# Layer 0's tile pipeline with the heads' normalization behind the second top-k round and the row statistics behind the third

## What is computed

```
x = x + attention(norm(x)) @ Wo + bo                      # projection: this stage
Q = norm(x) @ Wq.T + bq                                   # 16 heads
scores = Q K / 4                                          # 77 columns per head
topk_scores = top_k(scores, 32); weights = softmax(topk_scores)
x = x + (weights @ V) @ Wo.T + bo
h = norm(x); probs = softmax(h @ router_w + router_b)
x = x + (h @ expert_w[argmax].T + expert_b[argmax]) * max(probs)
```

## Time and profile before

| | |
|---|---|
| median of 3 runs | 1985.16 us (1983.98 to 1985.93) |
| the profiled execution, device time | 1987.05 us |
| its span in the trace | 1985.3 us |
| PE, DVE, ACT, POOL busy over the span | 80%, 63%, 47%, 24% |
| the stage cross_experts | 583.5 to 1118.5 us of the span |
| first top-k round starts | 608.10 us |
| distance of two tiles' first rounds, steady part | 27.24 us |
| tile 15's first round starts | 1006.21 us |
| last instruction of the stage | 1115.44 to 1116.07 us |

### The profile page before, as it was taken

How to read it: one execution, slowest core, us unless ns; L and a number is a source line. 1 busy time by engine, 2 the same in 40 slices (tenths; PEclk the granted TensorE clock), 3 DMA queues, 4 the chain that set the end, 5 groups by cost and what they waited for, 6 DMA issues and landing times. The chain is left out here.

```text
span 1985.3 us, 27618 instructions
## 1 busy us (share of the span) xinstructions
PE 1579.4 (80%) x8891; PEld 871.2 (44%) x8892; DVE 1255.1 (63%) x4695; ACT 934.1 (47%) x1831; POOL 482.1 (24%) x386
## 2 busy tenths in 40 slices
PE   4758999999976488889867676999987882389993
PEld 2431222222224366767656432333326761156662
DVE  6988888887407999999980356777735558401112
ACT  2731777777655445555543340666673651111110
POOL 3760000000003354455542151111111342300003
PEclk9965999999897778888878785999998995689997
DMA  6175133331010000000000059336300121741003
GB/s 196 59 203 79 21 45 44 44 45 20 25 43 1 1 1 2 1 1 1 1 1 1 6 163 170 43 44 86 44 1 1 15 41 32 254 162 33 26 24 93
DMA packets 113013, 102.91 MB, mean 52 GB/s; under 512 B 45095, under 2 KB 88171, under 8 KB 112878
## 3 DMA queue, kind: packets, MB, share of 16 engines
q1 hardware_dynamic: 111345, 97.06, 22.6%
q0 software_dynamic: 1536, 4.20, 0.7%
HBM read 67.61 MB, written 33.35 MB: 51 GB/s over the span
## 5 line engine op out<-in xcount | busy, mean ns | idle before, releaser
L1052 DVE TENSOR_REDUCE arena<-banks 128x2 f32<-128x1024 f32 (+1 forms) x448 | 481.2, 1108 | 149.7 <-PE banks L899 94.3
L988 ACT ACTIVATE arena<-banks 128x512 f32<-128x512 f32 (+3 forms) x896 | 439.9, 557 | 187.3 <-PE banks L938 180.6
L899 PE MATMUL banks<-arena 96*128 96x512 bf16 (+3 forms) x896 | 285.9, 396 | 50.1 <-DVE arena L1052 21.2
L938 PE MATMUL banks<-arena 98*128 98x512 bf16 (+3 forms) x896 | 272.0, 364 | 9.0 <-ACT arena L988 6.8
L950 PE MATMUL banks<-arena 128*32 128x512 f32 (+3 forms) x1792 | 220.8, 565 | 12.6 <-ACT arena L988 6.5
L1654 DVE MATCH_REPLACE8 arena<-arena 128x77 f32<-128x77 f32 x1024 | 213.9, 226 | 0.0
L899 PEld LDWEIGHTS banks<-arena 96*128 96x128 bf16 x896 | 80.6, 102 | 233.7 <-DVE arena L1052 136.9
L938 PEld LDWEIGHTS banks<-arena 98*128 98x128 bf16 x896 | 82.4, 98 | 188.0 <-ACT arena L988 124.1
L2433 DVE COPY arena<-banks 128x1024 f32<-128x1024 f32 x23 | 28.2, 1225 | 206.9 <-PE banks L2372 206.9
L1549 POOL TENSOR_SCALAR arena<-arena 128x256 f32<-128x256 f32 x32 | 39.1, 1223 | 476.2 <-DVE arena L1635 476.1
L1650 DVE MAX8 arena<-arena 128x8 f32<-128x77 f32 x1024 | 149.5, 225 | 1.4
(11 more groups left out here) (276 smaller groups left out, 2535.2 us busy)
## 6 DMA issues: line engine op xcount, KB each, us to landing
arena<-parts SPq DMA_DIRECT2D x192, 128.0 KB, 7.3
arena<-in_L_ffn_W SPq DMA_DIRECT2D x16, 1024.0 KB, 12.2
parts<-arena SPq DMA_DIRECT2D x24, 512.0 KB, 9.1
v<-arena SPq DMA_DIRECT2D x32, 256.0 KB, 2.3
arena<-v SPq DMA_DIRECT2D x16, 512.0 KB, 11.1
arena<-sorted SPq DMA_DIRECT2D x23, 128.0 KB, 2.1
expert_out<-arena SPq DMA_DIRECT2D x23, 128.0 KB, 1.7
sorted<-arena SPq DMA_DIRECT2D x5, 512.0 KB, 7.4
```

Of the source, the lines that this page charges most:

```text
L899: mm = pe.matmul(bank[:, 0:w], qst[r][0:KS, j, i * P:(i + 1) * P], kst[r][0:KS, j, kb * BANK:kb * BANK + w], start=True, stop=not diag)
L938: pe.matmul(bank, kst[r][0:KM, j, kt * P:(kt + 1) * P], qst[r][0:KM, j, half * BANK + lo:(half + 1) * BANK], start=True, stop=True).then_i ...
L988: act.activation(prob[:, gi % 2 * G + j, lo:BANK], PS[:, 4 + n % 3, 0:BANK - lo], ACT.Exp, scale=SCALE).then_inc(sem(s + "_exp"), 1)
L1052: dve.tensor_reduce(m2[u % 2][:, 2 * pair:2 * pair + 2, i, kb], PS[:, 2 * (n % 2):2 * (n % 2) + 2, 0:w], AX.X, ALU.max).then_inc(sem(s + " ...
```

## The change

An iteration now touches fewer tiles: t+2 (projection, first normalization), t+1 (queries and scores), t (top-k), t-1 (weights, context, heads' normalization, output, second normalization and logits) and t-2 (choice and experts). The loop runs from -2 to 17, 20 iterations. To make that possible within an iteration,

- DVE has `largest` split in two (the 8 largest; `taken`, the replacing). Its order is now: round 1; router, choose, chosen of t-2; round 2; `sums` and `normalize` of t-1; round 3; row statistics, gates; round 4; `inverse`.
- PE turns the weights of t-1, then context, turn_context, then choice and spread of t-2, then turn_mixed and output of t-1, experts of t-2, turn_h1, turn_h2, logits.
- ACT's order follows PE's; `deviations`, `gated`, `turned_h1`, `turned_h2` end its iteration.
- POOL does d2, w, the subtraction for all scores, the spread, then h2, h1, the bias and the addition to x.
- The experts' sum moves to bank 1 (EB), the logits to bank 7; the waits that guard banks and buffers follow. `choose` uses a two-tensor subtraction for the one with a scalar pointer. The eight expert matrices are turned 3, 3 and 2 at a time in the first iterations, before 2 in each of four. No DMA is added, removed or moved.

The arithmetic for each tile is the same.

```diff
-            PB, WB, QB, OB = 3, 4, 6, 7
-            FIRST, LAST = -3, T + 4
+            EB, PB, WB, QB, OB = 1, 3, 4, 6, 7
+            FIRST, LAST = -2, T + 2
+            TURNS = (3, 3, 2)
...
-                return [w for w, n in ((0, t + 2), (1, t - 3)) if inside(n)]
+                return [w for w, n in ((0, t + 2), (1, t - 1)) if inside(n)]
...
-                    if inside(t - 4):
-                        turn_choice(t - 4)
-                        turn_spread(t - 4, 0)
-                        turn_spread(t - 4, 1)
+                    if inside(t - 1):
+                        for c in range(4):
+                            turn_weights(t - 1, c)
+                        context(t - 1)
+                        turn_context(t - 1)
                     if inside(t - 2):
-                        turn_mixed(t - 2)
...
+                        turn_choice(t - 2)
+                        for c in range(4):
+                            turn_spread(t - 2, c)
+                    if inside(t - 1):
+                        turn_mixed(t - 1)
+                        output(t - 1)
...
+                        experts(t - 2, 0)
+                        experts(t - 2, 1)
                     if inside(t + 2):
                         turn_h1(t + 2)
-                    if inside(t - 3):
-                        turn_h2(t - 3)
                     if inside(t - 1):
-                        context(t - 1)
-                    if inside(t - 3):
-                        logits(t - 3)
+                        turn_h2(t - 1)
+                        logits(t - 1)
...
-                    dve.tensor_scalar(ta[n], lg[n], m1[n], None, ALU.subtract).then_inc(sem(s + "_ta"), 1)
+                    dve.tensor_tensor(ta[n], lg[n], m1[n].to_broadcast([P, E]), ALU.subtract).then_inc(sem(s + "_ta"), 1)
...
                 for t in range(FIRST, LAST):
-                    if inside(t - 4):
-                        router(t - 4)
+                    if inside(t):
+                        largest(t, 0)
+                        taken(t, 0)
+                    if inside(t - 2):
+                        router(t - 2)
+                        choose(t - 2)
+                        chosen(t - 2)
+                    if inside(t):
+                        largest(t, 1)
+                        taken(t, 1)
+                    if inside(t - 1):
+                        sums(t - 1)
+                        normalize(t - 1)
+                    if inside(t):
+                        largest(t, 2)
+                    if inside(t):
+                        taken(t, 2)
                     if normed(t):
                         row_statistics(t)
-                    if inside(t - 4):
-                        choose(t - 4)
-                    if normed(t):
                         aggregate(t)
...
```

More of the change, by code:

```diff
@@ L1176, in steps, with turned @@
                 return sum(1 for n in range(FIRST, t + 1) if normed(n))
+            def turned(t):
+                n = t - FIRST
+                return range(sum(TURNS[:n]), sum(TURNS[:n + 1]))
             @block.sync
@@ L1350, in _ @@
                         query(t + 1)
[L1351 to L1354, removed]
+                    if inside(t + 2):
+                        turn_attended(t + 2)
                     if inside(t + 1):
                         scores(t + 1)
[L1357 to L1361, removed]
@@ L1375, in _ @@
[L1375 to L1382, removed]
+                    if inside(t + 2):
+                        project(t + 2)
+                    for e in turned(t):
+                        turn_expert(e)
@@ L1500, in _ @@
                         exp_left(t - 1)
-                    if inside(t + 3):
-                        attended(t + 3)
-                    if inside(t - 4):
-                        router_exp(t - 4)
+                    if inside(t + 2):
+                        attended(t + 2)
+                    if inside(t + 1):
+                        copy_scores(t + 1)
+                    if inside(t + 2):
+                        attended_rows(t + 2)
+                    for e in turned(t):
+                        act.wait_ge(sem(s + "_wep"), e + 1)
+                        act.copy(WeT[:, e].rearrange("p k n -> p (k n)"), PS[:, WB + e % 2, :]).then_inc(sem(s + "_weT"), 1)
@@ new lines, in _ @@
+                    if inside(t - 1):
+                        for c in range(4):
+                            copy_weights(t - 1, c)
+                        context(t - 1)
+                    if inside(t - 2):
+                        router_exp(t - 2)
+                    if inside(t):
+                        exp_all(t)
+                    if inside(t - 2):
+                        choice(t - 2)
+                        for c in range(4):
+                            copy_spread(t - 2, c)
@@ L1505, in _ @@
+                    if inside(t - 1):
+                        mixed(t - 1)
+                        mixed_rows(t - 1)
                     if normed(t):
                         deviations(t)
[L1507 to L1514 removed]
@@ L1540, in _ @@
                     if inside(t - 1):
-                        context(t - 1)
+                        turned_h2(t - 1)
             @block.gpsimd
@@ L1650, in largest, with taken @@
                         dve.max(m8[r][:, k, hd, :], src[:, hd, :]).then_inc(sem(s + "_m" if k == 0 else f"{s}_m{k}"), 1)
+                def taken(t, k):
+                    r, hn = t % 2, t * NH
+                    src = (sc if k == 0 else left)[r]
                     dve.wait_ge(sem(s + "_m" if k == 0 else f"{s}_m{k}"), hn + NH)
```

157 lines of the change are left out of this document (57 added, 100 removed).

## The result

The changed kernel takes 2039.5 us (median of 4 runs, 2036.96 to 2046.45) against 1985.07 us: **2.8% slower**, ratio 1.0278, 95% interval 1.0262 to 1.0294. Forecast were 2043.5 us, range 2012 to 2070, slower.

A forecast was written before the change was run, and what follows sets the result against it. PE and DVE were both taken as close to the limit, with DVE newly waiting for context. Fill +3, distances +84.7 and tail -29 sum to +58.7 us, giving about 2043.5 us, range 2012 to 2070.

The forecast's parts named there:

- DVE's arrival and the chain: From round 4's end, DVE waits from 12.6 us for context arriving at 19.6; tile distance 33.0 us taken.
- The chain's last step: Context, ACT's copy of one bank, four turn_context transposes, tails and hops: from 16.6 to 19.6 us at the low clock.
- The queries and the table load: ACT's queries 0.63 us, then the unhidden table load 1.28 and exp_left 1.23, bring the chain to 10.6 us.
- the low clock for the logits and queries: PE's logits take 0.94 us and queries 2.05 at the low clock, against about 0.5 and 1.16 at the high one.
- a second gap of PE: PE idle from the scores until the weights come, besides the gap behind the experts; a reason for the low clock.
- the rival of a low clock that holds over the scores: Low clock lasts over scores, weights and experts: distance 35 us, time 2070 us; chance 0.13.
- Fill: Stage start to first round: +3 us, from three expert matrices ahead of h1 and `inverse` ahead of round 1.
- The second distance: Tiles 1 to 2, without h2 and logits in the chain: about 30 us.
- The tail: From tile 15's first round to the last addition: 80.6 us against 109.9, -29 us.
- the last one-hot to the end: Tail's final term, from the last one-hot to the stage's end: 19.2 us as before.
- the context never came in time: Opposite rival: context ready at about 12.3 us, ahead of DVE's 12.6; time 1938 to 1945 us; chance 0.04.
- no drain follows the load: Rival: a drain of about 1.38 us behind each ACT table load, time 2064 us; chance 0.02.

The follow-up runs named there:

- later-by-one-round kernel: Changed kernel with DVE's list alone altered, normalization behind round 3 and statistics behind round 4: 1985.64 us, ratio 0.9997 to the kernel before.
- exponential-first kernel: Changed kernel with ACT's exponential for the weights of t-1 ahead of the queries of t+1: 2033.3 us (one run).

## Why the prediction was right, point by point

- **DVE's arrival and the chain.** Both hold: arrival forecast at 12.6 us, measured 12.7 (876.48 less 6.67, from 857.1), context at 19.6 and 19.4. The distance was forecast as 33.0 and is 32.8 in the mean of the last 13. The later-by-one-round kernel shows that the place of the wait, and not the amount of work, makes the 54 us. (The chain's last step adds up to 19.8 us from its own terms, not 19.6.) In part the agreement is luck: the prediction never worked out when PE's own list, with scores and projection, reaches the weights. It came there 0.36 us before them. With slower scores that list would have set the distance, as it does in the tiles of 33.1 us of the exponential-first kernel.
- **Links.** The queries and the table load are on the chain as said, but with only 0.36 us to spare: taking the load out brought 0.5 us a tile and not 1.28. d2 is covered by them (863.27 against 865.38). The two orders with POOL or ACT alone altered moved the stage by +37.7 and -3.7 us, in the direction that the lists give.
- **The clock.** The forecast took the low clock for the logits and queries, and it was (1.02 and 2.05 us). One reason for it was wrong: I named a second gap of PE, from the scores until the weights come. It is 0.36 us, because the scores too ran at the low clock (3.77 us) and PE reached the weights just as they came (the rival of a low clock that holds over the scores came true so far; the weights and the experts ran at the high one). The clock fell with the first gap alone, and filling that gap kept it up.
- **The edges.** Fill +3.4 (forecast +3). 2.9 us of it went when the expert matrices were turned two at a time, one of the two causes given; what the other, `inverse` ahead of round 1, adds is not separated. The second distance is 29.7 (30). The tail is 77.6 instead of 80.6. In it, tile 15's rounds took 29.8 us and not 28, since tile 13's router between them was slow (its two-input steps took 2.26 and 2.30 us beside POOL's subtractions); the context took 15.2 us and not 17; and from the last one-hot to the end it was 16.6 us and not the 19.2 of before, mostly because PE's last experts took 7.2 us at the high clock where they had taken 9.2. The term was 3 us too large, the distances together 2.8 us. So the largest part of the tail's error is a clock that the forecast took over from one execution.
- **What the sum left out.** The stage before ended 4.9 us earlier in this execution and what comes behind took 2.3 us more. The changed kernel's runs spread over 9.5 us; those of the kernel before spread over 11.3 in the last comparison (1979.03 to 1990.31), so this is no property of the change. The forecast of the whole, 2043.5 against 2039.5, is 4 us too high where that of the stage is 5.6 too high.
- **Rivals.** In the middle part the context never came in time; no drain follows the load: the exponential starts at 866.68, 0.02 us behind the end of its load (865.38 + 1.28), and with no load at all the stage fell by 6.7 us only. On this the trace and the Trainium skill, page "ScalarE: Activation LUTs", section "What ACT_TABLE_LOAD costs", differ (it puts about 1.38 us there), and the trace decides.

## What to carry to other kernels

A shorter software pipeline saves iterations at the ends (29 us here, tail and fill together) but puts a chain into each iteration; before shortening, write down the chain from the last result of one tile to the first wait for it in the next, with every foreign instruction that stands ahead in each in-order list, and compare it with when the busiest engine arrives. Where the chain is late by less than one block of independent work, moving the wait behind one more block can give back the loss: here the distances fell by 58.6 us for 7.1 us more in the tail, which brought the time back to that of the kernel before, not below it. Altering the order of one engine on the chain without the others brought 38 us of loss or 4 us of gain.

## What the runs showed of the hardware

- The two DVE instructions of the choice, on 8 columns with two inputs in memory, take 0.17 and 0.22 us alone and up to 2.3 us beside a POOL instruction that reads two inputs; they end with POOL's. In the tail of the changed kernel both were hit:

```profile
1092.70 2.26 DVE L1584 TENSOR_TENSOR arena<-arena 128x8 f32<-128x8 f32 x1
1094.88 2.30 DVE L1585 SCALAR_TENSOR_TENSOR arena<-arena 128x8 f32<-128x8 f32 x1
```

  POOL's instructions there started at 1092.16 (2.78 us) and 1094.89 (2.26 us). DVE's top-k instructions beside the same POOL instructions keep their 0.22 us.
- A table load on ACT did not wait for the semaphore of the instruction that it serves: in the changed kernel the square root's load starts at 849.47, when ACT has nothing else to do, and the square root at 851.32 waits for DVE.

```profile
849.47 1.28 ACT L1413 ACT_TABLE_LOAD   x1
851.32 0.30 ACT L1413 ACTIVATE arena<-arena 128x2 f32<-128x2 f32 x1 [0.56 <-DVE arena L1611]
```

- 2.78 us of transposes in a gap of 3.1 us kept PE's queries at the high clock in the tile shown (1.14 us for 2.05), and the mean granted clock from 610 to 1000 us rose from 0.83 to 0.90.
